# Two fill tiles taken by turns in the later steps of the last layer, and edge attributes loaded after TensorE's first layer

## The reference

```
w = _kernel_net(edge_attr, kW1, kb1, kW2, kb2, kW3, kb3).reshape(-1, LATENT, LATENT)
...
for i in range(DEPTH):
    msg = jnp.einsum('ei,eio->eo', nodes[src], w)
    agg = jax.ops.segment_sum(msg, dst, num_segments=n)
    agg = agg * inv_deg
    nodes = jax.nn.gelu(agg + nodes @ root_W[i] + root_b[i])
```

## Time and profile before

| | us |
|---|---|
| median of three runs | 27579.13 |
| lowest and highest | 27549.18, 27592.92 |
| profiled execution, whole time | 27545.35 |
| its span, first to last instruction | 27543.6 |
| POOL busy | 22669.1 (82%) |
| PE busy | 22500.5 (82%) |
| DVE busy | 17653.1 (64%) |
| ACT busy | 14700.1 (53%) |

### The profile page before, as it was taken

How to read it: one execution, slowest core, us unless ns; L and a number is a source line. 1 busy time by engine, 2 the same in 40 slices (tenths; PEclk the granted TensorE clock), 3 DMA queues, 4 the chain that set the end, 5 groups by cost and what they waited for, 6 DMA issues and landing times. The chain is left out here.

```text
span 27543.6 us, 413278 instructions
## 1 busy us (share of the span) xinstructions
PE 22500.5 (82%) x110422; PEld 12380.9 (45%) x110422; DVE 17653.1 (64%) x29340; ACT 14700.1 (53%) x24676; POOL 22669.1 (82%) x30933
## 2 busy tenths in 40 slices
PE   7888848888879999968888886888868888688886
PEld 3444435555556666634444443333333333343333
DVE  5555548888878888844444444666656666566665
ACT  6666601111117777733333333777757777577775
POOL 7888868888868888878888888888878888788887
PEclk9999979999989999977777777999989889799888
DMA  3111135555542222222322323555545555455554
GB/s 89 34 34 34 39 59 94 92 94 93 93 83 74 75 75 76 75 76 96 97 96 96 97 95 92 163 163 163 163 129 165 163 163 163 129 168 162 163 162 127
DMA packets 2192590, 2964.46 MB, mean 108 GB/s; under 512 B 778166, under 2 KB 1678244, under 8 KB 2190948
## 3 DMA queue, kind: packets, MB, share of 16 engines
q1 hardware_dynamic: 1340898, 2776.49, 30.8%
q0 software_dynamic: 782304, 157.92, 8.7%
q10 hardware_dynamic: 69282, 28.92, 0.4%
HBM read 2289.02 MB, written 672.64 MB: 108 GB/s over the span
## 5 line engine op out<-in xcount | busy, mean ns | idle before, releaser
L772 POOL DMA_INDIRECT got<-table,idx x14040 | 13761.8, 980 | 3764.0 <-issue 3473.8
L790 PE MATMUL in_place<-place_hot,tparts 128*128 128x512 fp8e4 x49950 | 12164.8, 405 | 2750.4 <-ACT place_hot L995 2462.5
L995 ACT ACTIVATE place_hot<-place_b,far_lanes 128x512 fp8e4<-128x512 f16 x17550 | 10959.8, 704 | 12.3 <-PE in_place L790 11.3
L790 PEld LDWEIGHTS in_place<-place_hot,tparts 128*128 128x128 bf16 x49950 | 5076.0, 103 | 9118.6 <-issue 4170.7
L775 POOL MEMSET rest<- 128x256 f32 x14040 | 4686.2, 334 | 8.3
L1599 POOL DMA_INDIRECT added<-rows,add_idx x2160 | 3599.9, 1667 | 719.3 <-issue 655.2
L1171 DVE TENSOR_TENSOR prod<-w_in,rows_p 128x2048 f32<-128x2048 f32 x810 | 1853.1, 2288 | 2837.4 <-issue 1522.9
L1216 DVE TENSOR_TENSOR prod<-wcopy,got 128x1024 f32<-128x1024 f32 x810 | 968.6, 1223 | 2603.3 <-DMA got<-table,idx 2324.8
L1642 PE MATMUL acc<-hot,spread 128*128 128x392 bf16 x12960 | 2533.4, 349 | 0.0
L859 PE MATMUL wmat<-k,h 128*128 128x256 f32 x6480 | 2045.2, 446 | 0.0
L1225 DVE TENSOR_REDUCE msg<-prod 128x64 f32<-128x1024 f32 x1620 | 1969.0, 1215 | 41.4
(11 more groups left out here) (250 smaller groups left out, 23056.3 us busy)
## 6 DMA issues: line engine op xcount, KB each, us to landing
w_in<-kept SPq DMA_DIRECT2D x2430, 512.0 KB
kept<-wcopy SPq DMA_DIRECT2D x810, 512.0 KB
got<-table,idx POOLq DMA_INDIRECT x14040
attr<-in_edge_attr SPq DMA_DIRECT2D x270, 768.0 KB
place_b<-place_row SPq DMA_DIRECT2D x1350, 128.0 KB
range_b<-range_row SPq DMA_DIRECT2D x1350, 128.0 KB
rows<-in_src_row SPq DMA_DIRECT2D x270, 512.0 KB
sums<-outb SPq DMA_DIRECT2D x1350, 96.0 KB
```

The costliest lines, as they stand in the source:

```text
L772: pool.indirect_dma_start(out=got[:, r, j * W:(j + 1) * W], out_offset=None, in_=table, in_offset=bass.IndirectOffsetOnAxis(ap=idx[:, r, j ...
L790: mm = pe.matmul(in_place[b][:, h, :], tparts[:, s, t, :], place_hot[:, b, t, h * XC:(h + 1) * XC], start=(t == 0 and s == 0), stop=(t == ...
L995: ins = act.activation(place_hot[:, b, t, :], place_b[:, b, :], ACT.Abs_reciprocal_sqrt, bias=SB["far_lanes"][:, t:t + 1], scale=HOT_SLOPE ...
```

## The change

Two edits. In `kernel_kept` alone the fill tile `rest` has two halves that are taken by turns (`r % FILLS`), and the wait of a chunk is for the fills of two chunks before instead of one. In `kernel_net` the load of `attr` waits until TensorE has made layer 1 of all three groups of the chunk two before (`h1_made`), and VectorE's increments of `attr_used` are left out there.

```
-        rest = sb("rest", [P, J0 * RW])
+        FILLS = HALVES if kind == "kernel_kept" else 1
+        rest = sb("rest", [P, FILLS, J0 * RW])
...
                     if not first:
-                        if kind in ("relational", "kernel_net"):
+                        if kind == "relational":
                             sp.wait_ge(attr_used[b], i)
+                        if kind == "kernel_net":
+                            sp.wait_ge(S["h1_made"], (k - 1) * GROUPS)
...
-                    if at != 0:
-                        pool.wait_ge(S["rested"], k)
+                    if at is None or at >= FILLS:
+                        pool.wait_ge(S["rested"], k - FILLS + 1)
...
-                        ins = pool.memset(rest[:, j * RW:(j + 1) * RW], 0.0)
+                        ins = pool.memset(rest[:, r % FILLS, j * RW:(j + 1) * RW], 0.0)
...
-                    dve.sem_inc(attr_used[b], 1)
+                    if kind == "relational":
+                        dve.sem_inc(attr_used[b], 1)
```

## The result

The changed kernel is slower: median 27691.90 us against 27593.61 us of the kernel before on the same chip, ratio 1.0039 with the interval 1.0026 to 1.0052. The forecast was 27095, with a range of 27045 to 27220.

The account below looks back on a forecast made before the run. POOL was taken to bound the kernel, the rest waiting for it. Cheaper chunk ends in the later steps save 484 us, the first step's edit 0: 27579 - 484 = 27095 us, range 27045 to 27220 with rival 1.

Parts of the forecast that it names:

- POOL set the pace: Later steps: POOL works 2771.52 of 3322.20 us, 12.3 us a chunk, and never waits for the other engines.
- the 0.60 us: Later steps' chunk ends: cost falls from 0.77 to 0.17 us, saving 484 us over 807 ends.
- rivals 1 and 4: Later chunk ends: 1, they cost 0.31, time 27208, chance 0.08; 4, 0.60 is an increment's fixed price, 27579, chance 0.03.
- rival 2: Later steps: VectorE's scan holds gathers, 186 us (38 by chance), time 27281; also edit 2's upper bound, 27292; together 0.08.
- This needs the others to follow at 11.7 us: Later steps: other engines keep up with POOL's shorter chunk, their idle 2.1 to 3.5 us a chunk being enough.
- the landing of the gathers: Later steps: gathers in flight land late behind the burst of `w_in` loads; called the doubtful point in following at 11.7 us.
- VectorE's 941.4 us: Later step: VectorE's wait for ScalarE's copy of the gathered rows, 3.5 us a chunk, taken as idle time.
- the loop can do 10.2: Later steps: one turn between ScalarE's copies took 10.17 us; 11.7 needs fewer than four such turns in ten.
- POOL waits put down to indices: Later steps: a listed sign that the forecast is wrong, as the wait for indices was called far, three chunks ahead.
- Rival 3: Later steps: the burst becomes the bound at 12.55 us a turn, POOL stands at the ring; 194 us more, 27773, chance 0.03.
- Edit 2: First step's `attr` load: removes TensorE's wait for `attr`, 715 us off the path, so gain 0.
- shifted hits of VectorE's products on gathers: First step: gathers starting within a product take 1.68 instead of 0.95 us; 197 us either way, taken as 0.

Follow-up runs that it names:

- e15: Kernel before with the two fill tiles; in later steps from the fifth chunk every second gather becomes a 1004-column fill, wait behind first gather; 25956.74 us, ratio 0.9413.
- e5: Kernel before with the two fill tiles alone, and later-step fills 328 columns wide instead of 256; 27342.14 us, ratio 0.9914.
- e9: Kernel before, one fill tile, later steps' wait for the last fill moved behind the chunk's first gather, fills of 328 columns; 27410.12 us, ratio 0.9950.
- e6: Kernel before with one fill tile and the old wait, later-step fills 184 columns wide instead of 256; 27191.81 us, ratio 0.9859.
- e14: Kernel before with the two fill tiles alone, and later-step fills 312 columns wide instead of 256; 27333.22 us, ratio 0.9913.
- e1: Kernel before with the change's two fill tiles alone, without the attribute edit; 27673.52 us, ratio 1.0032.
- e8: Kernel before with the two fill tiles alone, later `w_in` loads cut to 64 columns a group, so no 1.5 MB burst; 27283.53 us, ratio 0.9892.
- e16: Kernel before with the two fill tiles alone; in later steps TensorE does 13 matmuls of 37 a chunk for `in_place`; 27255.29 us, ratio 0.9887.
- e7: Kernel before with the two fill tiles alone, the old wait for the last fill kept at every second chunk; 27321.72 us, ratio 0.9908.
- e17: Kernel before with one fill tile and the old wait, later-step fills 112 columns wide; 27716.85 us, ratio 1.0063.
- e11: Kernel before with the two fill tiles alone; each later step's third and fourth chunks wait for ScalarE's copy of the first and second; 27381.66 us, ratio 0.9941.

## Why the prediction was wrong

**What held.** POOL set the pace. The increment's wait was the 0.60 us, and where nothing else stops POOL the chunk end costs 0.17 (rivals 1 and 4 fall). The first half of rival 2 is smaller than even its lower case of 38 us: 342 gathers of the three later steps start within VectorE's scan and take 1.10 us, before 269 that took 1.08, which is some 15 us more, not 186. The kernel's other engines do have slack: with half of the gathers e15 has them at 10.33 us.

**The step that failed** is "This needs the others to follow at 11.7 us. ... I see it following." It took the others' idle time as theirs to give, independent of what POOL does, and looked for a limit only in the landing of the gathers. The landing was no limit: ScalarE's wait for rows went from 858.9 to 2.3 us. What the runs showed instead: 8 gathers in 11.7 us, one in 1.46, make TensorE's rows and signals and SP's transfers late, ScalarE and VectorE wait 824.4 and 772.0 us for TensorE, and these engines become the ones that set the pace, at 12.4 us a chunk, so that POOL stands at the ring. That lies above the 12.3 us that POOL needed before. Thinner gathers bring the signals back on time (e5, e9, e15). That signals as late as these must cost 12.4 us is not shown: e6 and e14 have them too and take 11.9 and 12.0.

The kernel before was at 1.538 us on average, but at 1.45 within a chunk, and its trace has late signals: within 6 us of POOL's last stand `in_row`'s signal was on time (0.01 us, 23 events), at 8 to 10 us it was 1.4 us late on average (88 events), and at 11 to 12 us, close to the next stand, 0.28 (78 events). The prediction never set TensorE's last row beside its waiter's start. Two readings in it were weak as well. Of VectorE's 941.4 us, 487.0 are put down to "issue" and not to ScalarE's copy, so they are not known to be slack. And "the loop can do 10.2" rests on one turn of 10.17 us between two long ones. One of its own signs of being wrong, POOL waits put down to indices, is what came.

**Rival 3** had the sign and the sight, a POOL that stands at the ring, with a chance of 0.03 and 194 us; e1 lost 91. Its mechanism is not what happened: it had gathers land behind the burst, and ScalarE hardly waits for gathers now. The burst does add to the price (e8), and its absence does not bring the signals back.

**Edit 2** was costed at 0 within 197 us either way by shifted hits of VectorE's products on gathers. It cost some 23 us (interval 0 to 0.18%): in gathers that the product holds longer, as that term said, and in fills that the copy into `outb` holds longer, which the term did not have. TensorE's wait for `attr` went away and gave nothing, as forecast. The Trainium skill, "SBUF — State Buffer", section "SBUF: two separate sides", has a two-input VectorE operation lock a GpSimd operation that reads SBUF out of a port pair that they share. The trace agrees for fills, whose rows name nothing that they read: within the product they take 0.33 us as elsewhere. Why the gathers are held there, no run shows apart.

**What stays open**: what TensorE and SP share with the gathers. e15 shows that it is the gathers' density, e8 and e16 that transfers and matmuls add to the price. For slow chunks the edge lies between 1.494 (e14) and 1.503 us a gather (e7), by one trace each of two kernels that differ in their stands too. Nor do the runs say why the price of gathers closer than that runs from 11.90 (e6) to 12.49 us a chunk (e17), or why a later start alone takes it from 12.41 (e1) to 12.03 (e11).

## What to carry to other kernels

Idle time of the engines that wait is slack only as long as the engine that is made faster takes nothing from them; before a pacing engine is sped up, set each producer's last record beside its waiter's start, and see whether the distance grows with the pace. Pauses between gathers are worth tuning by measurement, as the time does not fall steadily with them: here fills of 184 columns gained 1.4%, of 112 lost 0.6%, and taking every stand away lost 0.3% where taking every second gained 0.9%. When the profile names a releaser that has no business there, the trace's semaphore events tell the true one.

## What the hardware showed unexpectedly

Gathers of 128 rows delay other engines' signals and issues when they come densely. Evenly spaced at one in 1.507 us (e5) `in_row`'s signal comes 0.01 us behind its last row, at one in 1.494 us (e14) 6.30 us behind it. With a stand in each chunk and 1.45 us within it (before) it is 0.86 us. TensorE's rows and SP's transfers step with the starts of the gathers. TensorE's idle time ahead of `in_row` that is put down to nothing else ("issue") is 175.3 us in the third later step, before none; ScalarE's of that kind is 50 us, before 44. In e16 the granted clock in the later step is 0.66 where e1 has 0.89, with 13 matmuls of 37.
